# Layers 1 and 2: GpSimd's sum of x and bias waits for H's low part; layer 1's G product waits for two banks of the output sum

## The chip, the cores and the metric

One core of a Trainium2 chip runs the kernel. The metric is the device time in microseconds, the median of several runs.

## What is computed

Four layers, each `x = x + ffn(cond(x, style))`, on x of 32 x 64 x 1024 in float32.

```python
x = x + _L0_ffn_ref(_L0_cond_ref(x, cond_512, ...), L0_ffn_weight, L0_ffn_bias)
x = x + _L1_ffn_ref(_L1_cond_ref(x, cond_512, ...), L1_ffn_base_w, L1_ffn_base_b, L1_ffn_A, L1_ffn_B, L1_ffn_router_w)
x = x + _L2_ffn_ref(_L2_cond_ref(x, cond_512, ...), L2_ffn_W_base, L2_ffn_b_base, L2_ffn_W_router, ...)
x = x + _L3_ffn_ref(_L3_cond_ref(x, cond_512, ...), L3_ffn_U1, L3_ffn_V1, L3_ffn_U2, L3_ffn_V2, ...)
```

`cond` is a chain of four modulated one-dimensional convolutions over 64 channels (same, upsample with blur, same, blur with downsample), with per-sample scales from the style. The ffn of layer 0 is an fp8-quantised product, that of layer 1 a 1024 x 1024 product plus a top-2 mixture of 16 low-rank experts, that of layer 2 the same with a sparsemax over 8 experts of rank 16, that of layer 3 a gated low-rank network. The two layers that matter here:

```python
# layer 1
base_out = einsum('bsi,oi->bso', x, base_w) + base_b
res_hidden = einsum('bsi,ri->bsr', x, A)
logits = einsum('bsi,ei->bse', x, router_w)     # softmax, top 2
return base_out + einsum('bse,bsr,eor->bso', combine, res_hidden, B) * SCALING
# layer 2
weights = sparsemax(einsum('bsd,ed->bse', x, W_router) + b_router)
h = einsum('bsd,edr->bser', x, lora_A)
return einsum('bsd,od->bso', x, W_base) + b_base + einsum('bser,bse,ero->bso', h, weights, lora_B)
```

## The kernel before

The function `conv_phase` is built once for each layer. The batch is worked off in 16 pairs p of two samples (two halves h of one tile of 128 rows, each 512 columns). `over_pairs` gives each engine its own program over the pairs: pair 0 has code of its own, pairs 1 to 12 are a loop, pairs 13 to 15 are written out, with less and less work for the pairs ahead (`ahead` is 3, 2, 1, 0). The engines meet through counting semaphores alone. So the order of each engine's instructions is fixed by hand, and a wait holds everything queued behind it on that engine.

Every float32 operand of a product is split into a high part (written by ScalarE) and a low part (written by VectorE), and a product is three passes: hi x hi, hi x lo, lo x hi.

For a pair p in layers 1 and 2, in TensorE's order:

- `main_fast_half(p, 0)` (lines 1107 and 1117): the combined convolution of half 0, from the weight rows G (`l_g_hi`, `l_g_lo`), the "pairs" C, and the split of u.
- `weights_g(p + 1)` (line 1068): the product that makes the next pair's G, into PSUM banks 5 and 6. In the kernel before it waits for `xo_ready`: VectorE must have read the ffn result of pair p-1 out of banks 5, 6 and 7.
- `main_fast_half(p, 1)`, `conv0_half(p + 1, 0)` (line 1029), `transpose_h(p)` (line 1128, waits for GpSimd's `patch`), `conv0_half(p + 1, 1)`, `weights_a(p + 2)` (line 1043, into bank 2).
- `ffn(p)`: it waits for `hl_ready`, the low part of H. In layer 1 it is line 1152, 72 matmuls of 368 columns into banks 5, 6 and 7. In layer 2 it is the small product of line 1168 into bank 7, line 1186 into banks 5 and 6, with a transpose of the gated rows (line 1182) ahead of block 6, and line 1196, the experts' product, which waits for `l_gt_lo`.

VectorE for the same pair: `join_h` (line 1570, both halves), `sum_g` (line 1593), `sum_c` (line 1581, two instructions, both inputs in SBUF), `split_h` (line 1611, which writes H's low part and signals `hl_ready`; one input in PSUM), `split_g` (line 1599, two instructions, both tensor inputs in SBUF), `split_c` (line 1587), in layer 2 the sparsemax `gates` (lines 1725 to 1746), then `lead(p + 1)` (lines 1554 to 1564, 1537, 1529, 1518) and `tail(p)`. The tail of layer 1 first does `route(p - 1)` (lines 2021 to 2039, a chain of small instructions), then waits for the ffn product, copies the 80 small columns of bank 7 (line 1756, `small_read`), adds banks 5 and 6 to the row (line 1761, `x_part`), and adds the rest of bank 7 (line 1765, `xo_ready`). The tail of layer 2 writes `l_gt_lo` (line 1770) and, when the product is done, adds banks 5 and 6 to the row (line 1780).

ScalarE's `split_gc` writes G's and C's high parts (lines 1341 and 1342) behind `split_h`'s high part (line 1359). VectorE's line 1599 waits for the last of them.

GpSimd for each pair: `patch` (line 125, two small instructions), then the sum of the row of x and the bias in place (line 1990, 128 x 1024, both inputs in SBUF), which waits for the load `rows<-x`, and in layer 2 `take_edges` (line 125 on `XE`), which waits for the finished row. SyncE stores the row of pair p-1 when `xo_ready` comes, loads the next x, and when the store has landed loads the residual row of pair p (line 856).

Of the kernel before, what the change touches and what calls it, by code (L numbers as in the profile page):

```python
# [60 lines left out]
THIRD = (L + R1 + E1) // 3  # L61
REST = L - 2 * THIRD
# [40 lines left out]
def by_planes(t):  # L103

    return t.rearrange("p (m s) -> p s m", s=2)


def in_planes(t):
    return t.rearrange("p (s m) -> p s m", s=2)
# [513 lines left out]
def conv_phase(nc, layer, d, x_src, x_dst, pack, K, kept, sem, steps, ps):  # L623
# [7 lines left out]
    g0 = NP * layer  # L631
    n = layer + 1
    r0 = g0 - NP
# [4 lines left out]
    with ExitStack() as ctx:  # L638
        def sb(name, shape, dt=F32):
            return ctx.enter_context(nc.sbuf_tensor(lay + name, shape, dt))  # L640
# [41 lines left out]
        if with_ffn:  # L682
# [4 lines left out]
            else:  # L687
# [4 lines left out]
                small = sb("small", [P, SMALL[2]])  # L692
# [107 lines left out]
        t_done, hh_ready, hl_ready = sem("t_done"), sem("hh_ready"), sem("hl_ready")  # L800
# [19 lines left out]
        if with_ffn:  # L820
            bias_loaded, small_read, ffn_done, xr_loaded, xr_biased, xo_ready, x_stored = (sem(s) for s in (
                "bias_loaded", "small_read", "ffn_done", "xr_loaded", "xr_biased", "xo_ready", "x_stored"))
        if layer == 1:
            x_part = chain
# [138 lines left out]
        def _(pe):  # L963
# [86 lines left out]
            def weights_g(p):  # L1050

                pe.wait_ge(al_ready, 2 * (g0 + p) + 2)
                if with_ffn and not (isinstance(p, int) and p < 2):
                    pe.wait_ge(xo_ready, r0 + p - 1)
                for h in range(2):
                    k = 0
                    for ws, ms in PASSES:
                        for b in (0, 2):  # L1060
                            weights = c_part[ws][:, UT + (b + 1) * C:UT + (b + 3) * C]
                            if k < 2:
                                out, moving = ps[:, 5 + h, (b + b // 2) * C:(b + b // 2 + 5) * C], \
                                    As[0][:, h, b // 2 * C:(b // 2 + 5) * C]
                            else:
                                out = ps[:, 5 + h, (b + 1) * C:(b + 5) * C]
                                moving = As[1][:, h, :] if ms else As[0][:, h, C:5 * C]
                            mm = nc.tensor.matmul(out, weights, moving, start=(k == 0), stop=(k == 5),  # L1068
                                                  skip_group_check=True)
                            k += 1  # L1070
                    mm.then_inc(g_done, 1)
# [140 lines left out]
            def iteration(p, first, ahead):  # L1212
# [33 lines left out]
                if ahead:  # L1246
                    weights_g(p + 1)
# [258 lines left out]
        def _(dve):  # L1506
# [3 lines left out]
            v = nc.vector  # L1510
# [239 lines left out]
            def tail(p):  # L1750

                if layer == 1:
                    if not (isinstance(p, int) and p == 0):
                        route(nc, dve, kept, p - 1, sem)
                    dve.wait_ge(ffn_done, r0 + p + 1)
                    v.tensor_copy(kept["small"][:, :], ps[:, 7, REST:THIRD]).then_inc(small_read, 1)
                    dve.wait_ge(xr_biased, r0 + p + 1)
                    planes = in_planes(xr[:, :])
                    x2 = planes[:, :, 0:THIRD].rearrange("p s (c m) -> p s c m", c=2)
                    by_rest = planes[:, :, THIRD:HALF]  # L1760
                    v.tensor_tensor(x2, ps[:, 5:7, 0:THIRD].rearrange("p c (m s) -> p s c m", s=2), x2,
                                    ALU.add).then_inc(x_part, 1)
                    dve.wait_ge(x_part, r0 + p + 1)
                    dve.wait_ge(small_read, r0 + p + 1)
                    v.tensor_tensor(by_rest, ps[:, 7, 0:REST].rearrange("p (m s) -> p s m", s=2), by_rest,
                                    ALU.add).then_inc(xo_ready, 1)
                    return
                if layer == 2:
                    dve.wait_ge(side[2], side0[2] + p + 1)
                    v.tensor_tensor(gsp[1][:, :], ps[:, 7, 3 * P:4 * P], gsp[0][:, :].bitcast(F32),  # L1770
                                    ALU.subtract).then_inc(side[3], 1)
                    dve.wait_ge(side[3], side0[3] + p + 1)
                    v.tensor_copy(tau[:, 0:1], tau[:, 0:1]).then_inc(small_read, 1)
                if layer == 2 and isinstance(p, int) and p == NP - 1:
                    K.split_first_lo(nc, dve, 3, sem)
                if with_ffn:
                    dve.wait_ge(ffn_done, r0 + p + 1)
                    dve.wait_ge(xr_biased, r0 + p + 1)
                    x2 = xr[:, :].rearrange("p (s c m) -> p s c m", s=2, c=2)
                    v.tensor_tensor(x2, ps[:, 5:7, :].rearrange("p c (m s) -> p s c m", s=2), x2, ALU.add).then_inc(xo_ready, 1)  # L1780
# [144 lines left out]
        @block.gpsimd  # L1925
        def _(pool):
            def step(ins):
                steps["pool"](pool, ins)

            g = nc.gpsimd  # L1930
            step(g.memset(g_f[0:C, :, 0:C], 0.0))
            step(g.memset(g_f[C:P, :, TAPS7:HALF], 0.0))
            step(g.memset(As[0][:, :, 0:C].bitcast(F32), 0.0))
            step(g.memset(As[0][:, :, 5 * C:6 * C].bitcast(F32), 0.0))
            for t in Us:
                step(g.memset(t[:, :, 0:1].bitcast(F32), 0.0))
                last = g.memset(t[:, :, HALF + 1:HALF + 4].bitcast(F32), 0.0)
                if t is Us[1]:
                    last.then_inc(zeros_ready, 1)
                    pool.wait_ge(zeros_ready, 2 * layer + 1)  # L1940
                else:
                    step(last)
            step(g.memset(pe_f[:, :, :], 0.0))
            step(g.memset(EY[:, :, :, :], 0.0))
            if with_ffn:
                pool.wait_ge(sem(("q_stored1", "e_stored1")[layer - 1]), 8 * NP)
            g.memset(ve_f[:, :, :], 0.0).then_inc(zeros_ready, 1)
            def biased(p):

                pool.wait_ge(xb_loaded, 16 * (xb0 + p + 1))  # L1950
                g.tensor_tensor(xb[:, :], xb[:, :], last_bias[:, :], ALU.add).then_inc(xb_ready, 1)

            if layer == 0:
                pool.wait_ge(sem("l0_bias_loaded"), 16)
            if layer == 3:
                pool.wait_ge(sem("l0_bias_loaded"), 32)
                g.tensor_copy(in_planes(last_bias[:, :]), by_planes(xb[:, :])).then_inc(bias_ready, 1)
                pool.wait_ge(bias_ready, 1)

            def chunk(k):  # L1960
                pool.wait_ge(chunk_hi, ch0 + k + 1)
                g.tensor_tensor(chunks[k][1][1], staged(k), chunks[k][1][0].bitcast(F32),
                                ALU.subtract).then_inc(lo_by_pool, 1)

            if with_ffn:
                pool.wait_ge(bias_loaded, 16 * layer)
                step(g.tensor_copy(in_planes(bias[:, :]), by_planes(bias_n[:, :])))
            if len(chunks) > 0:
                pool.wait_ge(gl_ready, g0 + 1)
            for k in range(min(POOL_CHUNKS, len(chunks))):  # L1970
                chunk(k)
            pool.wait_ge(ey_ready, n)

            def patch(p):

                for h in range(2):
                    pool.wait_ge(hs_ready, 2 * (g0 + p) + h + 1)
                    carry_over(g, hs[:, h, :].rearrange("p (a b) -> p a b", b=2)[:, 0:HALF // 2:HALF // 2 - 1, :],
                               EY[:, 0:3:2, :, bass.ds(h * NP + p, 1)].rearrange("p s m a -> p s (m a)"),
                               ones[:, :]).then_inc(hs_patched, 1)  # L1980

            def iteration(p, first, ahead):
                patch(p)
                if layer == 0 and ahead:
                    pool.wait_ge(gl_ready, g0 + p + 2)
                if layer in (0, 3):
                    biased(p)
                if with_ffn:
                    pool.wait_ge(xr_loaded, 16 * (r0 + p + 1))
                    g.tensor_tensor(xr[:, :], xr[:, :], bias[:, :], ALU.add).then_inc(xr_biased, 1)  # L1990
                if layer == 2:
                    pool.wait_ge(xo_ready, r0 + p + 1)
                    take_edges(g, XE, p, xr[:, :], ones[:, :]).then_inc(xe_taken, 1)

            over_pairs(pool, iteration)


# [776 lines left out]
```

## Time and profile before

| what | value |
|---|---|
| median of 3 runs | 2101.85 us (2090.32 to 2104.71) |
| profiled execution: its own time | 2104.27 us |
| profiled execution: its span | 2102.1 us |
| mean granted TensorE clock | 0.982 |
| TensorE matmul busy | 1963.4 us, 93% |
| VectorE busy | 1302.0 us, 62% |
| ScalarE busy | 962.2 us, 46% |
| GpSimd busy | 377.8 us, 18% |
| pairs of layer 1 / layer 2 | about 390 to 755 us / 990 to 1400 us of the span |

The execution's own time lies 2.2 us above its span. Busy shares are averages over the whole span. The change touches two stretches only, so they have to be read by the timeline.

### The profile page before, as it was taken

What the parts mean: (1) busy time and instruction counts of PE and PEld (TensorE: products, weight loads), DVE (VectorE), ACT (ScalarE), POOL (GpSimd) and SP (SyncE); (2) the same over time, 40 slices, a digit from 0 to 9 for tenths busy, and PEclk for the clock granted to TensorE, in tenths of its full rate; (3) what the DMA queues carried; (4) which work ended last, traced back from release to release, by engine and by line L of the source; (5) the groups of instructions that cost most, each with busy time, mean ns of one, the idle gap of its engine ahead of it and who ended that gap; (6) DMA issues with size and microseconds to landing.
All of it is one profiled execution on the core that took longest, in us unless ns stands there. A gap on an engine that the chain in (4) does not pass through costs nothing. (4 is left out here: it accounts for less than half of the span.)

```text
span 2102.1 us, 32166 instructions
## 1 busy us (share of the span) xinstructions
PE 1963.4 (93%) x10207; PEld 1663.8 (79%) x10207; DVE 1302.0 (62%) x2326; ACT 962.2 (46%) x1547; POOL 377.8 (18%) x457
## 2 busy tenths in 40 slices
PE   5799968799999989998899999988999999999999
PEld 4688834799999978886788888877888878878886
DVE  6887878777776763327677666656555444444443
ACT  4488744455555431104344444434666544433441
POOL 4122211211111100002111111112121223322331
PEclk9999989999999999999999999999999999999999
DMA  7567547321112155444211122123233211142114
GB/s 195 172 196 193 175 164 242 96 70 60 60 62 88 51 176 159 136 135 143 74 59 60 60 62 73 56 69 118 100 100 109 86 50 45 53 143 87 46 45 163
DMA packets 118608, 222.30 MB, mean 106 GB/s; under 512 B 18336, under 2 KB 65184, under 8 KB 117792
## 3 DMA queue, kind: packets, MB, share of 16 engines
q1 hardware_dynamic: 102048, 212.36, 32.0%
q10 hardware_dynamic: 16512, 9.31, 1.6%
q8 instruction: 28, 0.46, 0.1%
q14 instruction: 20, 0.16, 0.0%
HBM read 159.04 MB, written 62.59 MB: 105 GB/s over the span
## 5 line engine op out<-in xcount | busy, mean ns | idle before, releaser
L2665 DVE SCALAR_TENSOR_TENSOR f_prod<-ps,b,f_gate 128x512 f32<-128x512 f32 (+1 forms) x88 | 66.1, 751 | 160.3 <-ACT f_gate L2605 160.3
L2706 POOL TENSOR_TENSOR x_lo<-f_prod,x_hi 128x512 fp32r<-128x512 f32 (+1 forms) x88 | 113.8, 1293 | 278.3 <-ACT x_hi L2612 278.3
L125 POOL TENSOR_TENSOR rows<-l_EY,ones 128x4 f32<-128x4 f32 x128 | 31.0, 242 | 730.0 <-ACT rows L1349 368.5
L2535 PE MATMUL ps<-pt_hi,v_hi 128*128 128x512 f32 (+1 forms) x352 | 137.5, 391 | 1.7 <-PEq L638 1.7
L2535 PE MATMUL ps<-pt_lo,v_hi 128*128 128x512 f32 (+1 forms) x352 | 137.3, 390 | 0.0
L2535 PE MATMUL ps<-pt_hi,v_lo 128*128 128x512 f32 (+1 forms) x352 | 137.2, 390 | 0.0
L2605 ACT ACTIVATE f_gate<-ps,b 128x512 f32<-128x512 f32 (+1 forms) x88 | 60.7, 690 | 156.0 <-PE ps L2535 156.0
L1570 DVE SCALAR_TENSOR_TENSOR rows<-ps,dem3e,l_middle 128x512 f32<-128x512 f32 x60 | 45.1, 752 | 121.4 <-ACT l_middle L1318 97.8
L125 POOL TENSOR_TENSOR XE<-rows,ones 128x8 f32 (+1 forms) x96 | 21.1, 243 | 533.6 <-DVE rows L1780 259.7
L1088 PE MATMUL ps<-l_u_hi,l_g_hi 128*128 128x512 f32 x272 | 111.5, 410 | 5.4 <-DVE l_g_lo L1604 5.2
L1088 PE MATMUL ps<-l_u_hi,l_g_lo 128*128 128x512 f32 x272 | 108.5, 399 | 0.0
L1088 PE MATMUL ps<-l_u_lo,l_g_hi 128*128 128x512 f32 x272 | 108.4, 398 | 0.0
L1029 PE MATMUL ps<-x_hi,c_hi 128*128 128x512 f32 x240 | 100.7, 420 | 0.0
L1593 DVE TENSOR_TENSOR l_g_f<-ps,l_g_f 128x1024 f32<-128x1024 f32 x64 | 78.1, 1220 | 34.5 <-ACT l_g_f L1327 34.5
L1029 PE MATMUL ps<-x_lo,c_hi 128*128 128x512 f32 x240 | 95.7, 399 | 0.0
L1029 PE MATMUL ps<-x_hi,c_lo 128*128 128x512 f32 x240 | 95.5, 398 | 0.0
L1518 DVE SCALAR_TENSOR_TENSOR x_lo<-xin,s_x,x_hi 128x512 fp32r<-128x512 f32 x120 | 85.0, 748 | 12.7 <-ACT x_hi L1281 12.6
L1326 ACT ACTIVATE l_g_f<-ps 64x896 f32<-64x896 f32 x64 | 58.7, 918 | 71.7 <-PE ps L1068 71.2
L1152 PE MATMUL ps<-l_w_hi,l_h_hi 128*128 128x368 f32 x384 | 87.0, 335 | 4.5 <-DVE l_h_lo L1611 4.5
L1990 POOL TENSOR_TENSOR rows<-rows,l_bias 128x1024 f32<-128x1024 f32 x32 | 78.4, 2451 | 63.2 <-DMA rows<-x 63.1
L1281 ACT ACTIVATE x_hi<-xin,s_x 128x512 fp32r<-128x512 f32 x120 | 81.1, 726 | 18.5 <-DMA xin<-in_x 18.5
L2612 ACT ACTIVATE x_hi<-f_prod 128x512 fp32r<-128x512 f32 (+1 forms) x88 | 55.8, 634 | 65.2 <-DVE f_prod L2665 65.2
(407 smaller groups left out, 5844.6 us busy)
## 6 DMA issues: line engine op xcount, KB each, us to landing
x<-rows SPq DMA_DIRECT2D x64, 512.0 KB, 2.9
xin<-x SPq DMA_DIRECT2D x96, 256.0 KB, 4.0
rows<-x SPq DMA_DIRECT2D x48, 512.0 KB, 4.1
out<-rows SPq DMA_DIRECT2D x32, 512.0 KB, 2.6
v<-in_ffn_v SPq DMA_DIRECT2D x84, 128.0 KB, 2.6
xin<-in_x SPq DMA_DIRECT2D x16, 512.0 KB, 6.1
xb<-in_x SPq DMA_DIRECT2D x16, 512.0 KB, 3.3
x<-xb SPq DMA_DIRECT2D x16, 512.0 KB, 2.6
```

Of the source, the lines that this page charges most:

```text
L1029: mm = nc.tensor.matmul(ps[:, h, :], c_part[ws][:, B0 + t * P:B0 + (t + 1) * P], Xs[ms][:, h, t:t + HALF], start=(k == 0), stop=(k == 5))
L1088: mm = nc.tensor.matmul(ps[:, 3 + h, :], Gs[ws][:, h, at:at + P], Us[ms][:, h, 1 + q:1 + q + HALF], start=(k == 0), stop=(k == 11))
L1152: mm = nc.tensor.matmul(ps[:, 5 + o, 0:THIRD], hsp[ws][:, b, :], wsp[ms][:, b, o * THIRD:(o + 1) * THIRD], start=(k == 0), stop=(k == 3 * ...
L1281: nc.scalar.activation(Xs[0][:, h, 1:HALF + 1], x_row(h), ACT.Copy, scale=column(s_x, p, h)).then_inc(xh_ready, 1)
L1326: nc.scalar.activation(g_f[0:C, :, C:HALF], ps[C:P, 5:7, 0:TAPS7], ACT.Copy).then_inc(g_crossed, 1)
L1518: v.scalar_tensor_tensor(Xs[1][:, h, 1:HALF + 1], x_row(h), column(s_x, p, h), Xs[0][:, h, 1:HALF + 1].bitcast(F32), ALU.mult, ALU.subtrac ...
L1593: v.tensor_tensor(g_f[:, :, :], ps[:, 5:7, :], g_f[:, :, :], ALU.add).then_inc(g_summed, 1)
L1990: g.tensor_tensor(xr[:, :], xr[:, :], bias[:, :], ALU.add).then_inc(xr_biased, 1)
L2535: mm = nc.tensor.matmul(ps[0:m, 2 * g + gu, :], v1sp[ws][:, s, r, gu, 0:m], pt[ms][:, r, cols], start=(k == 0), stop=(k == 5))
L2605: nc.scalar.activation(gate[0:m, g, :], ps[0:m, 2 * g, :], ACT.Silu, bias=b1[0:m, 0, bass.ds(2 * i + g, 1)]).then_inc(silu_ready, 1)
L2665: v.scalar_tensor_tensor(prod[0:m, g, :], ps[0:m, 2 * g + 1, :], b1[0:m, 1, bass.ds(2 * i + g, 1)], gate[0:m, g, :], ALU.add, ALU.mult).th ...
L2706: nc.gpsimd.tensor_tensor(asp[1][0:m, g, :], prod[0:m, g, :], asp[0][0:m, g, :].bitcast(F32), ALU.subtract).then_inc(al_ready, 1)
```

## The change

In layers 1 and 2 GpSimd waits for `hl_ready` of its pair before the sum of x and bias. In layer 1 the copy of the small columns moves behind the addition of banks 5 and 6, and `weights_g` waits for that addition's `x_part` and no longer for `xo_ready`. In layer 2 `weights_g` waits for `xo_ready` as before.

```diff
                 pe.wait_ge(al_ready, 2 * (g0 + p) + 2)
                 if with_ffn and not (isinstance(p, int) and p < 2):
-                    pe.wait_ge(xo_ready, r0 + p - 1)
+                    pe.wait_ge(x_part if layer == 1 else xo_ready, r0 + p - 1)
...
                     dve.wait_ge(ffn_done, r0 + p + 1)
-                    v.tensor_copy(kept["small"][:, :], ps[:, 7, REST:THIRD]).then_inc(small_read, 1)
                     dve.wait_ge(xr_biased, r0 + p + 1)
...
                     v.tensor_tensor(x2, ps[:, 5:7, 0:THIRD].rearrange("p c (m s) -> p s c m", s=2), x2,
                                     ALU.add).then_inc(x_part, 1)
+                    v.tensor_copy(kept["small"][:, :], ps[:, 7, REST:THIRD]).then_inc(small_read, 1)
                     dve.wait_ge(x_part, r0 + p + 1)
                     dve.wait_ge(small_read, r0 + p + 1)
...
                 if with_ffn:
+                    pool.wait_ge(hl_ready, g0 + p + 1)
                     pool.wait_ge(xr_loaded, 16 * (r0 + p + 1))
                     g.tensor_tensor(xr[:, :], xr[:, :], bias[:, :], ALU.add).then_inc(xr_biased, 1)
```

## Rows read from the trace of the kernel before

**Rows 1.** TensorE's waits: line, releaser, us in total, times, longest; 380:720, then 720:1420

```profile
PE ps L1152 <- DVE l_h_lo L1611: 2.1, 2, 1.1
...
PE ps L1168 <- DVE l_h_lo L1611: 13.7, 8, 2.8
```

**Rows 2.** Timeline of layer 1, one pair: start, us, engine, line, operation [idle before <-releaser]

```profile
566.90 2.41 POOL L1990 TENSOR_TENSOR rows<-rows,l_bias 128x1024 f32<-128x1024 f32 x1 [1.84 <-DMA rows<-x]
...
569.10 1.42 DVE L1599 SCALAR_TENSOR_TENSOR l_g_lo<-l_g_f,s_u,l_g_hi 128x512 fp32r<-128x512 f32 x2 [1.00 <-ACT l_pairs_hi L1342]
...
581.12 0.24 DVE L1756 COPY small<-ps 128x80 f32<-128x80 f32 x1
581.27 0.92 DVE L1761 TENSOR_TENSOR rows<-ps,rows 128x736 f32<-128x736 f32 x1
582.22 0.46 DVE L1765 TENSOR_TENSOR rows<-ps,rows 128x288 f32<-128x288 f32 x1
...
582.38 0.28 PE L1117 MATMUL ps<-l_u_hi,l_g_lo 128*128 128x256 f32 x1
582.83 0.53 PE L1068 MATMUL ps<-l_a_hi,c_hi 128*128 128x320 f32 x2 [0.17 <-DVE rows L1765]
```

**Rows 3.** Timeline of VectorE in layer 1: line 1611 of five pairs, line 1599 of one

```profile
426.33 1.21 DVE L1611 TENSOR_TENSOR l_h_lo<-ps,l_h_hi 128x1024 fp32r<-128x1024 f32 x1
...
473.31 1.23 DVE L1611 TENSOR_TENSOR l_h_lo<-ps,l_h_hi 128x1024 fp32r<-128x1024 f32 x1 [0.25 <-ACT l_h_hi L1359]
...
496.57 1.23 DVE L1611 TENSOR_TENSOR l_h_lo<-ps,l_h_hi 128x1024 fp32r<-128x1024 f32 x1 [0.25 <-ACT l_h_hi L1359]
...
498.80 1.69 DVE L1599 SCALAR_TENSOR_TENSOR l_g_lo<-l_g_f,s_u,l_g_hi 128x512 fp32r<-128x512 f32 x2 [1.00 <-ACT l_pairs_hi L1342]
...
520.11 1.23 DVE L1611 TENSOR_TENSOR l_h_lo<-ps,l_h_hi 128x1024 fp32r<-128x1024 f32 x1 [0.24 <-ACT l_h_hi L1359]
...
707.02 1.22 DVE L1611 TENSOR_TENSOR l_h_lo<-ps,l_h_hi 128x1024 fp32r<-128x1024 f32 x1 [0.25 <-ACT l_h_hi L1359]
```

**Rows 4.** Timeline of GpSimd and VectorE in layer 1, pair 13

```profile
707.80 2.41 POOL L1990 TENSOR_TENSOR rows<-rows,l_bias 128x1024 f32<-128x1024 f32 x1 [2.68 <-DMA rows<-x]
...
709.04 2.38 DVE L1599 SCALAR_TENSOR_TENSOR l_g_lo<-l_g_f,s_u,l_g_hi 128x512 fp32r<-128x512 f32 x2 [0.80 <-ACT l_pairs_hi L1342]
```

**Rows 5.** Timeline of layer 2, pair 7: VectorE, GpSimd, TensorE

```profile
1188.10 2.98 DVE L1581 TENSOR_TENSOR l_stage<-l_g_f 128x256 f32<-128x256 f32 x2
...
1188.39 2.41 POOL L1990 TENSOR_TENSOR rows<-rows,l_bias 128x1024 f32<-128x1024 f32 x1 [1.07 <-DMA rows<-x]
...
1192.27 0.40 PE L1168 MATMUL ps<-l_m,l_h_hi 128*128 128x272 f32 x1 [1.78 <-DVE l_h_lo L1611]
```

**Rows 6.** Timeline of layer 2, pair 6: VectorE and TensorE

```profile
1166.16 1.41 DVE L1599 SCALAR_TENSOR_TENSOR l_g_lo<-l_g_f,s_u,l_g_hi 128x512 fp32r<-128x512 f32 x2 [0.98 <-ACT l_pairs_hi L1342]
...
1177.76 0.29 DVE L1770 TENSOR_TENSOR l_gt_lo<-ps,l_gt_hi 128x128 fp32r<-128x128 f32 x1
...
1178.30 0.64 PE L1196 MATMUL ps<-l_b_hi,l_gt_hi 128*128 128x512 f32 x2
```

**Rows 7.** Timeline of GpSimd in layer 2: `take_edges` of pairs 2, 6, 7, 8, 14

```profile
1075.19 0.36 POOL L125 TENSOR_TENSOR XE<-rows,ones 128x8 f32 x2 [15.22 <-DVE rows L1780]
...
1181.33 0.36 POOL L125 TENSOR_TENSOR XE<-rows,ones 128x8 f32 x2 [15.36 <-DVE rows L1780]
...
1209.92 0.36 POOL L125 TENSOR_TENSOR XE<-rows,ones 128x8 f32 x2 [19.12 <-DVE rows L1780]
...
1235.04 0.36 POOL L125 TENSOR_TENSOR XE<-rows,ones 128x8 f32 x2 [15.36 <-DVE rows L1780]
...
1391.22 0.36 POOL L125 TENSOR_TENSOR XE<-rows,ones 128x8 f32<-128x8 f32 x2 [19.00 <-DVE rows L1780]
```

**Rows 8.** Stretches behind two waits of 1.78 us: busy by engine, PEclk, DMA share, GB/s

```profile
1194.00:1198.00 4.00, 4.00 (x14) 3.33 (x14) 3.65 (x16) 1.99 (x5) 0.00 (x0) 0.60 0.00 0
...
1323.00:1327.00 4.00, 4.00 (x21) 3.37 (x20) 3.69 (x15) 2.08 (x6) 0.00 (x0) 1.00 0.00 0
```

## Prediction

> **What bounds the kernel now.** I read the page's shares first: TensorE's matmuls are busy for 93% of the span, so only what opens or closes a gap on TensorE counts. Next comes the view of TensorE's waits over the two stretches that the change touches. In layer 1 the waits for H's low part reach 1.1 us at most, and there are two of them; in layer 2 there are eight, 13.7 us together [rows 1]. The waits say where a gap is, not what made the releaser late, so I then read the timeline of a pair engine by engine.
>
> In layer 1 the timeline shows VectorE at the edge. Behind line 1599 it runs its queue without a pause down to the copy of line 1756 and the two additions. TensorE's half 0 is issued to its end at 582.38, so the G product could start at about 582.50, one step of 0.12 later; it starts at 582.83, 0.15 behind line 1765's end (582.22 + 0.46) [rows 2]. That VectorE sets the pace is seen in the distance between one `l_h_lo` and the next: 496.57 - 473.31 = 23.26 us where line 1599 ran free, and 520.11 - 496.57 = 23.54 us where its two instructions took 1.69 us in place of 1.42 [rows 2, 3]. The extra 0.27 comes back whole in the interval.
>
> What lengthens line 1599 is GpSimd. In pair 13 the sum of x and bias starts at 707.80 and ends at 710.21; line 1599 starts at 709.04 and its pair of instructions takes 2.38, 0.96 more than free. So it got going at about 710.00, some 0.2 us before the sum's recorded end [rows 2, 4]. Both read two inputs from SBUF. In layer 2 the same happens one step earlier: in pair 7 the sum starts at 1188.39, between the two instructions of line 1581, and they take 2.98 us. H's low part is then late, and TensorE waits 1.78 us [rows 5]. Line 1611 itself has one input in PSUM and is 1.21 to 1.23 us long beside the sum and without it [rows 2, 3].
>
> The Trainium skill, "SBUF — State Buffer", section "Who interferes with whom", has this as a rule: a VectorE instruction with two SBUF inputs and a GpSimd instruction that reads SBUF take the same port, and the one that starts second is blocked for the other's whole length. The trace agrees on who is blocked. It differs a little on how long: held to the recorded end, each hold below would be 0.2 longer and the sum some 5 us higher, about 2115.
>
> **The change part by part.**
>
> *The wait on GpSimd.* It is behind `patch` and ahead of the sum; queued behind it are the sum and, in layer 2, `take_edges` and the next pair's `patch`. The sum is wanted by the tail's addition, more than 10 us later, so nobody waits for GpSimd's queue. What counts is where the sum now lies. It starts when `l_h_lo` ends, call that T, plus a handover. No row shows this very handover. From below it is 0; the nearest row has 0.15, from VectorE's line 1765 to TensorE [rows 2], and twice that, 0.3, is my upper bound. I take 0.17. VectorE comes to line 1599 at T + 1.00 in layer 1 and T + 0.98 in layer 2, since it waits for ScalarE's `l_pairs_hi` [rows 2, 6]. So GpSimd is first by 0.8 us, each time. The sum ends at T + 0.17 + 2.41 = T + 2.58, VectorE is free 0.2 before, at T + 2.39, and line 1599 is held 1.39 us. The bounds on the hold are 0 (nothing blocked) and 2.41 (the sum starting just ahead of line 1599).
>
> *Layer 1, VectorE's chain.* The whole chain moves by 1.39: the copy's place moves from 581.12 to 582.51. The addition of banks 5 and 6 now stands there, takes 0.92 and ends at 583.43; with the same 0.15 to TensorE the G product starts at 583.58 and not at 582.83 [rows 2]. So the second edit gives back 0.64 (the copy's 0.15 lead, the 0.46 of line 1765, and the steps between), and the first takes 1.39: 0.75 more, an interval of 24.01 against the free 23.26. From `l_h_lo` of pair 1 to that of pair 13 there are 12 intervals, 707.02 - 426.33 = 280.69 [rows 3]; 12 x 24.01 = 288.1, so +7.4 us. The interval behind pair 13 already has a hold of 0.96; with line 1599 only 0.80 behind T [rows 4] the new one is 1.6, and 1.6 - 0.96 - 0.64 is 0. In pair 1 the stall ahead of `l_h_lo` goes: -1.1 [rows 1]. Layer 1: +6.3 us.
>
> *The copy and the rest.* The copy and line 1765 now run while TensorE does the G product. `small_read` and `xo_ready` are next wanted by the coming ffn product and `route`, many us later. The store of the row and the loads behind it on SyncE's queue follow `xo_ready`, about 1.4 us later in the pair, of which 0.75 is the interval's own. The row is then loaded some 0.5 us before T, where GpSimd waits anyway (it started at 566.90 with T at 568.10, 1.2 before [rows 2]). So I cost this at nothing; where the load comes after T, the hold grows by as much.
>
> *Layer 2, what goes.* Six pairs (1, 3, 5, 7, 12, 14) have line 1581 blocked. The intervals of `take_edges` are 25.12 where nothing was blocked (1235.04 - 1209.92) and 28.59 in pair 7 (1209.92 - 1181.33). From pair 2 to pair 14 it is 316.03 for 12 intervals, and 12 x 25.12 = 301.4: 14.6 us go [rows 7]. Pair 1's wait adds 1.4 to that. Sum: -16.0.
>
> *Layer 2, what comes.* Behind line 1599 VectorE is again without a pause down to `l_gt_lo`, which ends at 1177.76 + 0.29 = 1178.05. TensorE's line 1196 starts at 1178.30 without a wait [rows 6]; the handover between the two is at least 0 and at most the 0.15 of [rows 2], I take 0.06, and the slack is 0.19. A hold of 1.41 leaves 1.2 us of waiting at line 1196. That is no longer one pair in two, but every pair from 1 to 13: 13 x 1.2 = +15.6. In pair 14, with less to do ahead, it is hidden. Net of layer 2: -0.4.
>
> *The sum.* 2104.27 + 6.3 - 0.4 = 2110.2. The profiled execution lies 2.4 above the median of the runs. I don't take that off: what differs from run to run is most likely how many pairs of layer 2 have the block, and that is what goes. I forecast 2110 us, with 2100 to 2122 as this case's own range.
>
> **The rivals.**
>
> *The clock falls too (slower).* TensorE now gets 26 waits, of about 1.1 us at line 1068 and 1.2 us at line 1196. Behind one wait of 1.78 in layer 2 the granted clock was 0.60 over 4 us, between its levels of 1.2 and 2.4 GHz; behind another of the same length it stayed 1.00 [rows 8]. One fall costs 4 x 0.40 = 1.6 us. If it follows on half of the new waits it adds 13 x 1.6 = 21: 2131. For it: the waits are periodic. Against it: they are shorter by a third, and even behind 1.78 it came only part of the time. It decides the matter from about eight falls on.
>
> *GpSimd blocks nothing there (faster).* Then layer 1 runs at the pace of TensorE, 23.26 - 0.33 = 22.93 for an interval: 280.69 - 275.2 = -5.5, with pair 1 -6.6; layer 2 gives its 16.0: 2104.3 - 22.6 = 2081.7. Against it stand both blocked rows [rows 4, 5]: there is no reason why line 1599 should be blocked in pair 13 and not in others.
>
> *Layer 2's hold is hidden.* If line 1196's three passes let it wait less (`l_gt_lo` is only wanted by the third, and weights and queue order may give more than the 0.19 that I read), layer 2 keeps its 16.0 and only layer 1 pays: 2104.3 + 6.3 - 16.0 = 2094.6. A wait stands ahead of all three passes in the program, which speaks against it.
>
> **How the numbers follow.** Forecast 0.60, clock 0.15, nothing blocked 0.12, hidden in layer 2 0.13. A measurement of this kernel can tell about 1% from no change. The forecast's range and the hidden case lie within 1% of 2101.85 (2081 to 2123), apart from its upper edge. Faster by over 1%: half of the "nothing blocked" case, 0.07. Slower: most of the clock case and the forecast's upper edge, 0.15. Within 1%: 0.78. The range of 2090 to 2132 holds the forecast, the hidden case and half of the clock case.
>
> **What would show it.** In the new profile every L1990 of pairs 1 to 14 starts 0.1 to 0.3 behind the end of L1611. L1599's two instructions take 2.8 in place of 1.42. L1581 is at 0.76 throughout. TensorE's view of waits has about 13 of 1.2 us at L1196 (released by `l_gt_lo`), about 13 of 1.1 us at L1068 released by line 1761, and no wait of over 1 us at L1168 in pairs 1 to 14. Layer 1's intervals are 24.0, layer 2's 26.3. L1599 at 1.42 with the sum beside it would fell the forecast; PEclk under 0.9 over layer 2's pairs would mean the clock case; L1196 without waits the hidden one.

## The result, and the profile after

The changed kernel takes 2111.45 us (median of 6 runs, 2109.49 to 2113.41), against 2100.97 us for the kernel before beside it (6 runs, 2090.32 to 2104.71). The ratio is 1.0059, 95% interval 1.0035 to 1.0084: slower by 0.6%, inside the 1% that a measurement of this kernel can hardly tell from nothing, but clear of its interval. The forecast was 2110.

The page of the changed kernel: the span, and busy us of each engine.

```profile
span 2111.2 us, 32191 instructions
...
PE 1960.8 (93%) x10199; PEld 1660.5 (79%) x10207; DVE 1325.2 (63%) x2326; ACT 958.4 (45%) x1547; POOL 377.4 (18%) x457
```

TensorE's work is what it was. VectorE is "busy" for 23 us more with the same 2326 instructions: that is waiting inside an instruction, which the profile counts as busy. TensorE's waits in the changed kernel, 380 to 730 us and then 720 to 1430 us (line, releaser, us in total, times, longest):

```profile
PE ps L1068 <- DVE rows L1760: 10.8, 12, 0.9
...
PE ps L1152 <- DVE l_h_lo L1611: 1.0, 1, 1.0
...
PE ps L1196 <- DVE l_gt_lo L1770: 20.0, 14, 6.3
...
PE ps L1168 <- DVE l_h_lo L1611: 3.4, 3, 1.4
```

This is [rows 1] after the change. In layer 2 the 13.7 us of waiting for H's low part have gone down to 3.4, and a wait for `l_gt_lo` stands in their place, 14 times, of which the long one (6.3) is pair 0's and was there before as 6.7. In layer 1 the G product now waits 0.9 us in each of the twelve pairs of this stretch, though it waits for two banks only.

One pair of layer 1, timelines of GpSimd, VectorE and TensorE (the answer to [rows 2]; line 1760 is the addition of banks 5 and 6, line 1762 the copy, and the sum of x and bias is line 1991 now):

```profile
570.07 1.23 DVE L1611 TENSOR_TENSOR l_h_lo<-ps,l_h_hi 128x1024 fp32r<-128x1024 f32 x1 [0.24 <-ACT l_h_hi L1359]
...
571.46 2.41 POOL L1991 TENSOR_TENSOR rows<-rows,l_bias 128x1024 f32<-128x1024 f32 x1 [3.20 <-DVE l_h_lo L1611]
...
572.29 2.80 DVE L1599 SCALAR_TENSOR_TENSOR l_g_lo<-l_g_f,s_u,l_g_hi 128x512 fp32r<-128x512 f32 x2 [1.00 <-ACT l_pairs_hi L1342]
...
585.60 0.28 PE L1117 MATMUL ps<-l_u_hi,l_g_lo 128*128 128x256 f32 x1
...
585.69 0.93 DVE L1760 TENSOR_TENSOR rows<-ps,rows 128x736 f32<-128x736 f32 x1
586.53 0.23 DVE L1762 COPY small<-ps 128x80 f32<-128x80 f32 x1
...
586.76 0.53 PE L1068 MATMUL ps<-l_a_hi,c_hi 128*128 128x320 f32 x2 [0.89 <-DVE rows L1760]
586.87 0.46 DVE L1765 TENSOR_TENSOR rows<-ps,rows 128x288 f32<-128x288 f32 x1
...
594.07 1.22 DVE L1611 TENSOR_TENSOR l_h_lo<-ps,l_h_hi 128x1024 fp32r<-128x1024 f32 x1 [0.25 <-ACT l_h_hi L1359]
```

Read it from the top. H's low part is done at 571.30; GpSimd's sum starts 0.16 later. Line 1599 comes 1.00 behind, as before, and now takes 2.80 in place of 1.42. It comes loose at about 573.67, 0.2 before the sum's end at 573.87. The G product starts 0.14 behind the addition's end, at 586.76 where it could have started at 585.72 (the view counts 0.89 of waiting and not 1.04, because it starts at the end of the matmul before). The interval from one line 1611 to the next is 24.00.

One pair of layer 2 in the same way (the answer to [rows 6]):

```profile
1197.14 1.23 DVE L1611 TENSOR_TENSOR l_h_lo<-ps,l_h_hi 128x1024 fp32r<-128x1024 f32 x1 [0.27 <-ACT l_h_hi L1359]
...
1198.55 2.40 POOL L1991 TENSOR_TENSOR rows<-rows,l_bias 128x1024 f32<-128x1024 f32 x1 [3.21 <-DVE l_h_lo L1611]
1199.35 2.82 DVE L1599 SCALAR_TENSOR_TENSOR l_g_lo<-l_g_f,s_u,l_g_hi 128x512 fp32r<-128x512 f32 x2 [0.98 <-ACT l_pairs_hi L1342]
...
1212.36 0.29 DVE L1770 TENSOR_TENSOR l_gt_lo<-ps,l_gt_hi 128x128 fp32r<-128x128 f32 x1
1212.70 0.74 PE L1196 MATMUL ps<-l_b_hi,l_gt_hi 128*128 128x512 f32 x2 [1.08 <-DVE l_gt_lo L1770]
```

Line 1581 is at 0.76 for its two instructions in every pair now. The hold has moved from there to line 1599, and the wait on TensorE from line 1168 to line 1196.

The distances from one line 1611 to the next, read off VectorE's timeline. They are the measure of all that follows:

| kernel | layer 1, pairs 1 to 13, mean of 12 | layer 1, pairs 0 to 15 | layer 2, usual interval | layer 2, pairs 0 to 15 | median us |
|---|---|---|---|---|---|
| before, first profile | 23.39 | 355.9 | 25.13, six pairs with a block | 400.6 | 2100.97 |
| changed | 24.01 | 360.9 | 26.47 | 399.8 | 2111.45 |

### The profile page after: what moved, and what is told of

It is laid out like the page before. It is cut to its first block and busy times, and to the rows that moved or that the text cites. A ratio compares the mean times of both kernels' runs of the same rounds, so it can differ in the third digit from the quotient of the medians.

```text
span 2111.2 us, 32191 instructions
## 1 busy us (share of the span) xinstructions
PE 1960.8 (93%) x10199; PEld 1660.5 (79%) x10207; DVE 1325.2 (63%) x2326; ACT 958.4 (45%) x1547; POOL 377.4 (18%) x457
## 5 line engine op out<-in xcount | busy, mean ns | idle before, releaser
L1599 DVE SCALAR_TENSOR_TENSOR l_g_lo<-l_g_f,s_u,l_g_hi 128x512 fp32r<-128x512 f32 x64 | 85.2, 1370 | 33.1 <-ACT l_pairs_hi L1342 31.3
```

The source lines that it names most:

```text
L1599: last = v.scalar_tensor_tensor(Gs[1][:, h, :], g_f[:, h, :], column(s_u, p, h), Gs[0][:, h, :].bitcast(F32), ALU.mult, ALU.subtract)
```

## Experiments

All but three kernels (the wait alone, and the kernel before twice more) are the changed kernel with one edit. Where a kernel has one run, what is read from it are the lengths and distances in its trace, not its time.

### GpSimd's wait alone

```diff
# against the kernel before
+                    pool.wait_ge(hl_ready, g0 + p + 1)
                     pool.wait_ge(xr_loaded, 16 * (r0 + p + 1))
```

> The kernel before with GpSimd's wait for H's low part alone; layer 1's G product waits for the whole output sum as before. My theory: line 1599 is held 1.39 us in each pair of both layers, and nothing gives 0.64 back in layer 1. Layer 1's interval from one line 1611 to the next is 23.26 + 1.39 = 24.65 us (the changed kernel has 24.01), layer 2's is 26.47 as in the changed kernel. 13 x 0.64 = 8.3 us above the changed kernel: about 2120 us, ratio to before about 1.009. Rival (the second edit gives nothing, TensorE's 24.01 is set by something else): 24.01 and about 2111 us.

Measured: 2121.96 us (4 runs; the kernel before 2098.8), ratio 1.0107 (1.007 to 1.0143). Layer 1's intervals from pair 1 to pair 13 are 24.58 to 24.64, layer 2's 26.42 to 26.52. TensorE's waits in layer 1 of this kernel:

```profile
PE ps L1068 <- DVE rows L1765: 18.5, 13, 1.5
```

The hold of 1.39 is added whole to the free interval of 23.26. The second edit is worth 24.63 - 24.01 = 0.62 us in each pair, where 0.64 was forecast. In layer 1 from pair 0 to pair 15 that is 367.9 - 360.9 = 7.0 us. The medians differ by 10.5; some 3 us of it lie outside the pairs of both layers, where the two kernels are all but the same.

### The second edit alone

```diff
# against the changed kernel
-                    pool.wait_ge(hl_ready, g0 + p + 1)
```

> The changed kernel without GpSimd's wait: only layer 1's order of the copy and the wait for two banks. My theory: layer 1's chain on VectorE is 23.26 - 0.64 = 22.62 us plus whatever hold line 1599 has, so TensorE's 22.93 sets most intervals; layer 2 is as before, with line 1581 blocked in some pairs and intervals of 25.1 to 28.6. 12 x (23.39 - 22.95) = 5 us less than before: about 2096 us, ratio about 0.9975. Rival (the second edit is worth nothing): 2101 us and intervals as before. Rival (a shorter interval brings the row's load later against line 1611, and the hold grows): intervals of 23.1 to 23.4 and about 2099 us.

Measured: 2097.5 us (10 runs) against 2098.8, ratio 0.9996 (0.9974 to 1.0017): no difference that can be told. Layer 1's intervals behind pairs 2 to 12 are 22.87 to 23.71. The timelines of GpSimd and VectorE in this kernel show why they aren't all 22.9:

```profile
591.07 1.22 DVE L1611 TENSOR_TENSOR l_h_lo<-ps,l_h_hi 128x1024 fp32r<-128x1024 f32 x1 [0.25 <-ACT l_h_hi L1359]
...
591.80 2.42 POOL L1990 TENSOR_TENSOR rows<-rows,l_bias 128x1024 f32<-128x1024 f32 x1 [2.54 <-DMA rows<-x]
...
593.30 2.13 DVE L1599 SCALAR_TENSOR_TENSOR l_g_lo<-l_g_f,s_u,l_g_hi 128x512 fp32r<-128x512 f32 x2 [1.00 <-ACT l_pairs_hi L1342]
```

The sum starts 0.5 before line 1611's end and not 1.2 before it as in [rows 2]. In both kernels it starts 7.1 to 7.9 us behind the end of line 1765, because store and load of the row take that long; but line 1611's end now lies 8.0 behind line 1765 and not 8.7. The sum reaches further into line 1599, whose pair takes 1.61 to 2.50 in these. This is the third case of the expectation. What the second edit gives, the hold eats: the mean interval from pair 1 to pair 13 is 23.36, and 23.34 to 23.39 in three profiles of the kernel before.

### The sum behind VectorE's chain

```diff
                 if with_ffn:
-                    pool.wait_ge(hl_ready, g0 + p + 1)
+                    if layer == 1 and ahead:
+                        pool.wait_ge(gl_ready, g0 + p + 2)
+                    elif layer == 2 and ahead:
+                        pool.wait_ge(side[0], side0[0] + p + 1)
+                    else:
+                        pool.wait_ge(hl_ready, g0 + p + 1)
                     pool.wait_ge(xr_loaded, 16 * (r0 + p + 1))
```

> The changed kernel, but GpSimd's sum waits longer: in layer 1 for the end of line 1587 (gl_ready of the next pair), in layer 2 for the end of the sparsemax chain. Behind both VectorE has 2.04 us of instructions that have one input in PSUM or a short one, then line 1529 and line 1560 with two inputs in SBUF. My theory: the sum starts 0.17 behind, VectorE is free 2.39 behind, so the hold is 0.35 at line 1529 in place of 1.39 at line 1599. Layer 1's interval 22.97 us, layer 2's 25.3 us (slack of 0.19 at line 1196), together 13 x 1.04 + 13 x 1.17 = 29 us less than the changed kernel: about 2083 us, ratio about 0.991. Rival (any busy time of GpSimd beside VectorE costs, whatever the operands): intervals stay at 24.0 and 26.5 and the time at 2111 us. Rival (line 1596's other costs, not the sum, set the intervals): the same.

Measured: 2082.47 us (5 runs) against 2098.8, ratio 0.9919 (0.989 to 0.9948). Layer 1's interval is 23.05, layer 2's 25.50. Timelines of VectorE and GpSimd in layer 1 of this kernel (the sum is line 1996):

```profile
588.13 0.88 DVE L1587 SCALAR_TENSOR_TENSOR l_pairs_lo<-b_raw,s_u,l_pairs_hi 128x256 fp32r<-128x256 f32 x2
...
588.99 0.69 DVE L1555 TENSOR_TENSOR c_raw<-ps,l_middle 128x510 f32<-128x510 f32 x1
...
589.18 2.44 POOL L1996 TENSOR_TENSOR rows<-rows,l_bias 128x1024 f32<-128x1024 f32 x1 [6.41 <-DVE l_pairs_lo L1587]
589.59 0.68 DVE L1556 TENSOR_TENSOR c_raw<-ps,l_middle 128x512 f32<-128x512 f32 x1
590.19 0.87 DVE L1537 SCALAR_TENSOR_TENSOR l_a_lo<-ps,s_p,l_a_hi 128x256 fp32r<-128x256 f32 x2
590.97 1.19 DVE L1529 SCALAR_TENSOR_TENSOR z_lo<-Z,s_v,z_hi 128x192 fp32r<-128x192 f32 x2
```

Lines 1555, 1556 and 1537 lie wholly or mostly beside the sum and keep the lengths that they had without it (0.68, 0.68, 0.86): each has one of its tensors in PSUM. The first with both in SBUF, line 1529, is held 0.45 (1.19 in place of 0.74). The same instruction of GpSimd, placed 3.2 us later in layer 1 and 6.8 later in layer 2, costs 0.2 and 0.4 in a pair (against 22.88 and 25.12 below) and not 1.1 and 1.35. The time is 29 us below the changed kernel's and was forecast to 1 us.

### A sum of 8 columns

```diff
-                    g.tensor_tensor(xr[:, :], xr[:, :], bias[:, :], ALU.add).then_inc(xr_biased, 1)
+                    g.tensor_tensor(xr[:, 0:8], xr[:, 0:8], bias[:, 0:8], ALU.add).then_inc(xr_biased, 1)
```

> The changed kernel with GpSimd's sum cut to 8 of 1024 columns (the bias is left out of the other columns). My theory: with no sum to hold line 1599, layer 1's interval is TensorE's 22.93 us and layer 2's 25.12, 13 x 1.08 + 13 x 1.35 = 32 us less than the changed kernel: about 2080 us, ratio about 0.990. Rival (the semaphore wait itself, or the late row, makes the intervals long): 24.0 and 26.5 stay, 2111 us.

Measured: 2074.48 us (4 runs), ratio 0.9885 (0.9848 to 0.9922). Layer 1's interval is 22.88, layer 2's 25.12, line 1599's pair 1.42. All waits of the changed kernel are still there. So neither they nor a late row make the intervals: the sum over 1024 columns does. In pairs 1 to 12 TensorE has no wait for VectorE left, so these two intervals are TensorE's own pace, and the floor for any placing of the sum. It came out 5 us lower than forecast. From pair 0 to pair 1 layer 1 takes 23.87 us here and 27.41 in the changed kernel: a cost of the sum in pair 0 that I hadn't seen (below).

### Writing only

```diff
-                    g.tensor_tensor(xr[:, :], xr[:, :], bias[:, :], ALU.add).then_inc(xr_biased, 1)
+                    g.tensor_tensor(xr[:, 0:8], xr[:, 0:8], bias[:, 0:8], ALU.add)
+                    g.memset(xr[:, 8:HALF], 0.0)
+                    g.memset(xr[:, HALF:L], 0.0).then_inc(xr_biased, 1)
```

> The changed kernel with GpSimd writing zeros over 1016 of the row's 1024 columns in two memsets, behind a sum of 8 columns; x and bias are left out of those columns. GpSimd is still busy from line 1611's end, but reads nothing from SBUF. My theory (the hold is over reading a second input from SBUF): line 1599's pair stays at 1.42 us wherever the memsets run beside it, intervals 22.9 and 25.1, about 2075 us. Rival (any GpSimd instruction holds VectorE's): line 1599's pair is longer by as much as the memsets reach past its start, and the intervals too. If the memsets end before line 1599 starts, this run says nothing on it.

Measured: 2077.16 us (one run), line 1599's pair 1.41 or 1.42. The memsets (0.52 and 0.53 us) end 0.3 behind line 1599's start, and with the 0.2 that the hold always ends early, only 0.1 of a hold could have shown. That overlap was too short to tell, so a second run put the memsets later, behind four sums of 8 columns:

```diff
+                    for k in range(0, 32, 8):
+                        g.tensor_tensor(xr[:, k:k + 8], xr[:, k:k + 8], bias[:, k:k + 8], ALU.add)
+                    g.memset(xr[:, 32:HALF], 0.0)
+                    g.memset(xr[:, HALF:L], 0.0).then_inc(xr_biased, 1)
```

> As the run with two memsets, but behind four sums of 8 columns, so that the memsets run from about 0.8 to 1.8 behind the end of line 1611 and line 1599 starts in their midst, at 1.00. My theory (the hold is over reading from SBUF): line 1599's pair stays at 1.42. Rival (any GpSimd instruction holds it): its pair takes 2.0, held to the memsets' end less 0.2.

Measured: 2072.52 us (one run). Timelines of GpSimd and VectorE:

```profile
604.93 0.68 POOL L1992 TENSOR_TENSOR rows<-rows,l_bias 128x8 f32<-128x8 f32 x4 [3.20 <-DVE l_h_lo L1611]
605.54 0.50 POOL L1993 MEMSET rows<- 128x480 f32 x1
...
605.75 1.42 DVE L1599 SCALAR_TENSOR_TENSOR l_g_lo<-l_g_f,s_u,l_g_hi 128x512 fp32r<-128x512 f32 x2 [0.99 <-ACT l_pairs_hi L1342]
605.98 0.53 POOL L1994 MEMSET rows<- 128x512 f32 x1
```

Line 1599 starts with a memset running and another behind it, for 0.76 us together, and takes its 1.42. A GpSimd instruction that only writes does not hold it.

### Two halves

```diff
+                    g.tensor_tensor(xr[:, 0:HALF], xr[:, 0:HALF], bias[:, 0:HALF], ALU.add)
+                    g.tensor_tensor(xr[:, HALF:L], xr[:, HALF:L], bias[:, HALF:L], ALU.add).then_inc(xr_biased, 1)
```

> The changed kernel with the same sum as two instructions of 512 columns, one behind the other. My theory (each instruction holds for its own length, and a waiting GpSimd instruction gets in between two of VectorE's, as in the kernel before at line 1581): the first half holds line 1599's first instruction to 1.2 behind the end of line 1611, that is by about 0.2, the second half gets in between its two and holds the second for 1.2: together about 1.4, intervals of 24.0 and 26.5 and about 2111 us, no gain. Rival (VectorE keeps its turn for both instructions): 0.2 alone, intervals of 22.9 and 25.2, about 2077 us.

Measured: 2110.52 us (one run), intervals 23.95 and 26.4. Timelines of GpSimd and VectorE:

```profile
595.41 1.31 POOL L1991 TENSOR_TENSOR rows<-rows,l_bias 128x512 f32<-128x512 f32 x1 [3.20 <-DVE l_h_lo L1611]
596.24 2.75 DVE L1599 SCALAR_TENSOR_TENSOR l_g_lo<-l_g_f,s_u,l_g_hi 128x512 fp32r<-128x512 f32 x2 [1.00 <-ACT l_pairs_hi L1342]
596.70 1.74 POOL L1992 TENSOR_TENSOR rows<-rows,l_bias 128x512 f32<-128x512 f32 x1
```

The second half takes 1.74 where the first takes 1.31: it waits for line 1599's first instruction, and then goes ahead of its second. Line 1599's pair is 2.75, almost as long as with one long sum (2.80). Cutting the instruction alone gives nothing, because the two engines take turns.

### One input

```diff
+                    g.tensor_tensor(xr[:, 0:8], xr[:, 0:8], bias[:, 0:8], ALU.add)
+                    g.tensor_scalar(xr[:, 8:L], xr[:, 8:L], 1.0, 1.0, ALU.mult, ALU.mult).then_inc(xr_biased, 1)
```

> The changed kernel with GpSimd's sum replaced by a product with 1.0 of the row in place: one input from SBUF in place of two (the bias is left out of 1016 columns). My theory: it holds line 1599 as well, to about 0.2 before its own end; how much the interval grows follows from how long it is. If it takes 2.4 us: 24.0 and 26.5; if it takes 1.2 us: hold 0.4, intervals of 23.0 and 25.4. Rival (only two inputs against two inputs meet): line 1599's pair stays at 1.42 beside it.

Measured: 2080.21 us (one run), intervals 22.89 and 25.25. Timelines of GpSimd and VectorE:

```profile
608.42 1.04 POOL L1992 TENSOR_SCALAR rows<-rows 128x1016 f32<-128x1016 f32 x1
609.09 1.58 DVE L1599 SCALAR_TENSOR_TENSOR l_g_lo<-l_g_f,s_u,l_g_hi 128x512 fp32r<-128x512 f32 x2 [1.00 <-ACT l_pairs_hi L1342]
```

With one input the instruction takes 1.04 us and not 2.41, ends at 609.46, and line 1599 is held 0.16, to 609.25: again 0.2 before the end. So one SBUF input on GpSimd's side is enough for a hold. In layer 1 a hold of 0.16 is free, since VectorE's chain has 22.62 + 0.16 against TensorE's 22.88; in layer 2 the hold is 0.20 and costs 0.13.

### Two windows

```diff
                     pool.wait_ge(hl_ready, g0 + p + 1)
                     pool.wait_ge(xr_loaded, 16 * (r0 + p + 1))
-                    g.tensor_tensor(xr[:, :], xr[:, :], bias[:, :], ALU.add).then_inc(xr_biased, 1)
+                    cut = 384
+                    g.tensor_tensor(xr[:, 0:cut], xr[:, 0:cut], bias[:, 0:cut], ALU.add)
+                    if layer == 1 and ahead:
+                        pool.wait_ge(gl_ready, g0 + p + 2)
+                    elif layer == 2 and ahead:
+                        pool.wait_ge(side[0], side0[0] + p + 1)
+                    g.tensor_tensor(xr[:, cut:L], xr[:, cut:L], bias[:, cut:L], ALU.add).then_inc(xr_biased, 1)
```

> The changed kernel with the sum cut in two: 384 columns start when H's low part is written, the other 640 behind line 1587 in layer 1 and behind the sparsemax chain in layer 2. My theory: the first part takes 0.95 us and is done with its reads at 0.17 + 0.95 - 0.2 = 0.92 behind line 1611, before line 1599 starts at 1.00; the second takes 1.55 and ends before line 1529 starts 2.04 behind. No hold at all: line 1599's pair 1.42, line 1529's pair 0.74, intervals of 22.9 and 25.1 as with the sum cut away, and about 2075 to 2077 us, ratio about 0.989. Rival (what the sum costs is not the place where it lies but that it is there): 2083 us as with the whole sum behind the chain, or more.

Measured: 2076.73 us (4 runs) against 2096.79, ratio 0.9899 (0.9864 to 0.9934). Layer 1's interval is 22.89, layer 2's 25.22. Timelines of GpSimd and VectorE:

```profile
603.98 1.04 POOL L1992 TENSOR_TENSOR rows<-rows,l_bias 128x384 f32<-128x384 f32 x1 [3.20 <-DVE l_h_lo L1611]
604.80 1.43 DVE L1599 SCALAR_TENSOR_TENSOR l_g_lo<-l_g_f,s_u,l_g_hi 128x512 fp32r<-128x512 f32 x2 [0.99 <-ACT l_pairs_hi L1342]
...
607.10 1.60 POOL L1997 TENSOR_TENSOR rows<-rows,l_bias 128x640 f32<-128x640 f32 x1 [2.08 <-DVE l_pairs_lo L1587]
609.00 0.73 DVE L1529 SCALAR_TENSOR_TENSOR z_lo<-Z,s_v,z_hi 128x192 fp32r<-128x192 f32 x2
```

Both parts lie where VectorE is idle or reads PSUM, and lines 1599 and 1529 are held by 0.06 at most in the usual pair. Layer 2's interval is still 0.10 above the floor; what makes it was not looked into. This does the whole sum and is within 3 us of the kernel that leaves it out. It beats the kernel before by 1.0%, and by the medians the changed kernel by 1.6% (2076.73 to 2111.45).

### The kernel before, twice more

> The kernel before once more, for its trace. Theory: its time from run to run follows the number of pairs of layer 2 in which line 1581 is blocked; the first profile has six of them, and each costs 2.1 to 3.5 us in the intervals from one line 1611 to the next. So this profile's layer 2 from pair 0 to pair 15 is 400.6 us less about 2.7 for each block fewer than six. Rival (the spread of the runs comes from elsewhere): the same number of blocks or the same 400.6 us at another time.

> The same again: layer 2's pairs take 400.6 us less about 2.7 for each block fewer than six; rival: no such relation.

Measured: 2102.84 and 2102.05 us. In both, line 1581 is blocked in four pairs of layer 2 and not in six, and layer 2 from pair 0 to pair 15 takes 393.6 and 394.5 us; 400.6 - 2 x 2.7 = 395.2 was forecast. The run with the second edit alone, whose layer 2 is that of the kernel before, has four blocks as well, and 395.7 us. So layer 2's time goes with the count of blocks, as far as two counts can show it. How much a block costs goes with the clock behind it: pair 7 of the first profile, with a granted clock of 0.60, costs 3.5 us over its two intervals, pair 12, with 1.00, costs 2.1 [rows 8].

The count doesn't set the kernel's time: the spans, 2100.7 and 2099.9, are only 1.4 and 2.2 below the first profile's 2102.1. Layer 1 (356.4 and 358.5 against 355.9) and the stretches outside the two layers took back the rest. In both, line 1581 is blocked in pair 14 of layer 1 too, which the first profile doesn't have.

## Why the prediction was right

**The sum's new place.** Forecast: 0.17 behind line 1611, ahead of line 1599 by 0.8, in each pair. Measured 0.16 to 0.18 in pairs 1 to 12 of both layers, where the hold was forecast as 1.39 and is 1.37 to 1.41. In pairs 13 and 14, which are written out, it is mostly 0.08, outside the 0.1 to 0.3 that the prediction gave as a sign, and in pair 13 of layer 1 it is 0.38: there the row's load came last, and line 1599 is held 1.79 where 1.6 was forecast. That case had been named and costed at nothing; it came once and cost some 0.2 us. The two experiments that move the sum away and cut it down show that it is the cause.

**The rule of the page.** The Trainium skill, "SBUF — State Buffer", section "Who interferes with whom", says that a VectorE instruction with two SBUF inputs contends with a GpSimd instruction that reads SBUF but not with one that only writes it, and that one with a single SBUF input, outside the modes that use both port pairs, doesn't contend. The traces agree on each count: lines 1599 and 1529 with two SBUF inputs are held (2.80 for 1.42, 1.19 for 0.74), lines 1555, 1556 and 1537 with one are not; a GpSimd instruction with one SBUF input holds (1.58 for 1.42); one that only writes doesn't (1.42). On the length the measurement differs, as the prediction had said: the hold ends 0.2 us before the recorded end.

**Layer 1.** Forecast for an interval 24.01, measured 24.01; from pair 1 to pair 13 the forecast was 288.1 and the trace has 288.07. That VectorE's chain sets the pace, that the hold goes into it whole and that the second edit takes 0.64 off again is each shown by a kernel (24.63 with the wait alone, 22.88 without the hold). From pair 0 to pair 15 the layer grew by 5.0 and not 6.3. The mis-sized term is pair 0 to pair 1: forecast -1.1, measured 27.41 - 29.96 = -2.55. Here are the 12 us that start 12 behind line 1611 of pair 0, in the first and second profile of the kernel before and in the changed kernel (busy by engine, PEclk, DMA share, GB/s):

```profile
408.37:420.37 12.00, 9.08 (x49) 8.78 (x49) 7.96 (x16) 5.24 (x7) 0.20 (x1) 0.72 0.31 88
```

```profile
411.21:423.21 12.00, 8.72 (x62) 8.11 (x62) 8.17 (x16) 6.80 (x9) 0.20 (x1) 1.00 0.29 89
```

```profile
410.58:422.58 12.00, 9.12 (x59) 8.81 (x59) 7.93 (x15) 6.49 (x9) 0.20 (x1) 0.86 0.28 89
```

In each, TensorE waits 2.9 us at line 1107 for `l_u_lo`. Behind that wait the granted clock was at its lower level for part of the stretch in the first profile (0.72) and in the third (0.72), where pair 0 to pair 1 takes 29.96 and 29.93; it stayed up in the second (1.00), which takes 26.69; in the changed kernel it was 0.86 and 27.41. In the first and third, line 1581 of pair 1 comes 27.7 us behind line 1611 of pair 0 and meets the sum; in the second it comes at 25.7, ahead of it. So what the change took away there, the kernel before doesn't always have: against its second profile the changed kernel is 0.7 slower in this place, not 2.55 faster. The share of the clock and that of the block were not separated.

**Layer 2.** What went was forecast as 16.0, what came as 15.6, a net of -0.4. Against the first profile the measured net is 399.83 - 400.56 = -0.7. The run with 8 columns, with neither block nor hold, has 382.56, so what went is 400.56 - 382.56 = 18.0 and what came 399.83 - 382.56 = 17.3. Both sides of that sum were off, by 2.0 and 1.7, and the errors cancelled: the net was met by luck. The gain was low in pair 0 to pair 1, which went from 35.95 to 33.07 where I had put 1.4. The price was low because the interval is 26.47 where 25.12 + 1.2 = 26.3 was forecast, and the term of the sum behind it is the slack of 0.19. Line 1196 does start 0.05 behind `l_gt_lo` in place of 0.25; but behind the wait its first two matmuls take 0.74 us together and not 0.64 [rows 6]. Holds of 1.41, 0.44 and 0.20 (the changed kernel, the sum behind the chain, one input) cost 1.35, 0.38 and 0.13 in an interval: the slack is 0.06 to 0.07.

**The total.** The two layers explain 5.0 - 0.7 = 4.3 us, against 5.9 forecast. The profiled executions differ by 2113.41 - 2104.27 = 9.1. The remaining 4.8 lie outside these stretches: 2.2 ahead of layer 1's first line 1611, 1.6 between the layers, 1.0 behind. Of what the change touches, they hold only the end of pair 15 of each layer. The three profiles of the kernel before alone differ by 2.8, 1.5 and 0.7 in these places. The 1.6 goes with the clock: from 36 to 46 us behind line 1611 of pair 15 of layer 1 the granted clock is 0.83 in the changed kernel and 1.00 in the first profile, but 0.83 as well in the second profile of the kernel before, which takes 245.8 between the layers like the changed kernel's 245.9 (244.3 in the first). The other two I take for spread; that wasn't tested by itself. The forecast of 2110 was helped by all three.

**Against the runs.** I did not take off the 2.4 us by which the profiled execution lay above its median, on the ground that the count of blocks makes the spread. That ground is only half shown. Layer 2 follows the count, the whole time doesn't. What holds is that the first profile's layer 2, with six blocks, is the slow end: two others had 393.6 and 394.5, and against those the changed kernel's 399.8 is a loss of 5 to 6 us. That fits with a measured difference of medians, 10.5 us, that is larger than a sum made on that one profile, but it doesn't show the reason: the two profiled executions with four blocks took 2102.84 and 2102.05, above the median of 2100.97 themselves. From that median the 5.9 us of the forecast would have led to 2106.9. So the intervals were forecast well, and the last 3 us of the number were luck. The changed kernel's own runs lie within 4 us of each other, the kernel before's within 14.

**The rivals.** The clock did not fall behind the new waits of 0.9 and 1.1 us: layer 2's stretch from 1044 to 1400 us has a granted clock of 1.00 after the change, and 0.99 before it, where it had fallen behind waits of 1.78 [rows 8]. Layer 1's from 420 to 740 us has 1.00 in both.

```profile
1044.00:1400.00 356.00, 341.33 (x1944) 294.39 (x1943) 251.78 (x571) 143.63 (x257) 42.12 (x67) 1.00 0.18 56
```

GpSimd does block in each pair. Layer 2's hold was not hidden: line 1196 waits 1.08.

## What to carry to other kernels

Moving a GpSimd instruction that reads SBUF is moving a hold on VectorE: look at what VectorE runs for the next two microseconds at the new place, and which of it has both inputs in SBUF. The good places are those where VectorE is idle or reads PSUM, and the instruction can be cut so that each part fits its place; cutting it without moving the parts gives nothing. An irregular stall in some pairs can be cheaper than a small one in each: multiply both by their counts before trading one for the other.

## What was not expected

- Line 1628 of pair 0 in layer 1, which splits the weights, has two SBUF inputs as well. Three instructions of it take 5.69 us beside the sum in the changed kernel, 5.71 in the first profile of the kernel before (so the change didn't bring this), and 3.49 in the run with 8 columns. With the sum moved behind the chain, pair 0 to pair 1 goes from 27.41 to 24.21 us, with 8 columns to 23.87. Most of the 5 us by which that run beat its forecast are these 3.5, of which about 0.7 go with the clock (27.41 against 26.69 above).
- GpSimd and VectorE take turns by instruction: a GpSimd instruction that waits goes ahead of the second of two VectorE instructions queued back to back (line 1581 in the kernel before, the two halves here).
- On GpSimd the float32 sum of two inputs took 2.41 us for 1024 columns and a product with one input 1.04 us for 1016, as long as a sum of two inputs over 384. The length of the hold follows the number of inputs as much as that of columns.
